# One-hot slot tables of a mixture-of-experts stage: two-byte operands, batches innermost, slot numbers laid out once

## The reference, cut to what matters

```python
capacity = max(1, int(CF * N / E))              # 560 slots of each expert
probs = jax.nn.softmax(xf @ router_w.T, axis=-1)
topw, topi = jax.lax.top_k(probs, K)            # K = 2 experts for each of 3584 tokens
order = jnp.lexsort((-fw, fe))                  # by expert, then by weight
rank = jnp.arange(N * K) - starts[se]
keep = rank < capacity
disp = zeros.at[se, pos].set(xf[st])[:, :capacity]     # the rows of x that each expert gets
g, u = einsum(disp, wg), einsum(disp, wu)
eo = einsum(silu(g) * u, wd)
out = zeros.at[st].add(eo[...] * weight)
```

## Time and profile before

| | us |
|---|---|
| median of 3 runs | 3769.72 |
| lowest, highest | 3767.74, 3772.16 |
| the profiled execution, its own time | 3775.88 |
| its span | 3774.1 |

### The profile page before, as it was taken

How to read it: one execution, slowest core, us unless ns; L and a number is a source line. 1 busy time by engine, 2 the same in 40 slices (tenths; PEclk the granted TensorE clock), 3 DMA queues, 4 the chain that set the end, 5 groups by cost and what they waited for, 6 DMA issues and landing times. The chain is left out here.

```text
span 3774.1 us, 84215 instructions
## 1 busy us (share of the span) xinstructions
PE 3639.7 (96%) x28244; PEld 3139.7 (83%) x28244; DVE 2361.0 (63%) x5543; ACT 1731.9 (46%) x4278; POOL 1305.9 (35%) x1388
## 2 busy tenths in 40 slices
PE   8999999999979999999999999849999999999999
PEld 7888888888868888888888888638998899989998
DVE  6888888888846666666666666576433434434343
ACT  4555555555435555555555555413333333333332
POOL 2333333333325656666556566510101101011010
PEclk9999999999989999999999999869999999999999
DMA  4222222222243434444434343223324334234232
GB/s 127 60 54 63 54 63 53 64 53 64 72 122 94 112 106 104 108 116 107 121 96 113 104 108 97 71 68 94 121 82 122 107 98 123 82 118 123 85 108 69
DMA packets 315057, 349.72 MB, mean 93 GB/s; under 512 B 45308, under 2 KB 232036, under 8 KB 314884
## 3 DMA queue, kind: packets, MB, share of 16 engines
q1 hardware_dynamic: 305796, 318.26, 30.7%
q0 software_dynamic: 9088, 29.17, 2.4%
HBM read 183.23 MB, written 38.91 MB: 59 GB/s over the span
## 5 line engine op out<-in xcount | busy, mean ns | idle before, releaser
L1627 DVE TENSOR_REDUCE x_mx<-x_psS 112x1 f32<-112x752 f32 x512 | 479.7, 937 | 382.2 <-PE x_psS L1180 378.6
L2423 DVE TENSOR_TENSOR hid<-e_psU,act_g 128x280 f32<-128x280 f32 x256 | 115.1, 450 | 622.6 <-PE e_psU L34 585.8
L1462 ACT ACTIVATE x_pt<-x_psE 125x448 f32<-125x448 f32 x768 | 389.6, 542 | 227.6 <-PE x_psE L1192 217.7
L1051 POOL TENSOR_TENSOR part<-x_pt 125x448 f32<-125x448 f32 x255 | 292.4, 1147 | 506.0 <-ACT x_pt L1462 497.1
L2049 POOL DMA_INDIRECT out<-ex_y,sidx x40 | 39.8, 995 | 1020.4 <-DVE ex_y L2457 1010.2
L635 POOL TENSOR_TENSOR qks<-qks,cos 128x448 f32<-128x448 f32 x128 | 148.1, 1157 | 657.0 <-DMA qks<-qk 657.0
L1180 PE MATMUL x_psS<-k_st,q_st 97*112 97x376 f32 x1024 | 287.9, 362 | 24.1 <-DMA k_st<-mk 16.3
L32 PE MATMUL e_psG<-ex_hi,g_hi 128*128 128x280 f32 x1024 | 304.2, 297 | 6.7 <-ACT act_g L2208 4.5
L32 PE MATMUL pj<-xT_hi,win_hi 128*128 128x224 f32 x1024 | 302.2, 295 | 4.0 <-PEq L185 3.9
L2208 ACT ACTIVATE act_g<-e_psG 128x280 f32<-128x280 f32 x256 | 103.7, 405 | 426.4 <-PE e_psG L34 412.1
L1053 POOL TENSOR_TENSOR part<-part,x_pt 125x448 f32<-125x448 f32 x255 | 292.3, 1146 | 20.0
(11 more groups left out here) (305 smaller groups left out, 10890.3 us busy)
## 6 DMA issues: line engine op xcount, KB each, us to landing
k_st<-kT SPq DMA_DIRECT2D x768, 93.8 KB, 2.2
raw_g<-in_L_ffn_wg SPq DMA_DIRECT2D x128, 256.0 KB
raw_u<-in_L_ffn_wu SPq DMA_DIRECT2D x128, 256.0 KB
raw_d<-in_L_ffn_wd SPq DMA_DIRECT2D x128, 256.0 KB
qks<-qk SPq DMA_DIRECT2D x512, 56.0 KB, 2.0
q_st<-qT SPq DMA_DIRECT2D x384, 56.0 KB, 2.0
ctxt<-in_ctx SPq DMA_DIRECT2D x16, 1125.0 KB
xt<-in_x SPq DMA_DIRECT2D x16, 448.0 KB, 3.7
```

Source lines behind the costliest of these rows:

```text
L1051: pool.tensor_tensor(part[:], pt[j][:, 0, :], pt[j][:, 1, :], ALU.add).then_inc(parted, 1)
L1462: act.activation(pt[j][:, i, :], psE[(j + i) % 2][0:KR, 0:2 * T], ACT.Exp, scale=XD ** -0.5).then_inc(exp_done, 1)
L1627: dve.tensor_reduce(mx[:, j, h:h + 1], psS[0:HT, :, 0:376], AX.XY, ALU.max).then_inc(s_taken, 1)
L2423: dve.tensor_tensor(h[ring][:, halves[s]], psU[:, 0:CH], act_g[i][:, halves[s]], ALU.mult).then_inc(S["mul"], 1)
```

## The change

`lo` becomes a two-byte tile (its values, 1 to 128, are exact in bfloat16). A new tile `slot_no` of 128 x 16 two-byte elements on each partition holds the slot numbers, each 16 times in a row; ScalarE writes it once, behind `same`. `onelo` is laid out with the batches innermost, so `one_low` compares two two-byte operands whose innermost step is one element, where before it compared two four-byte operands that were both spread out. In exchange the stationary operand of a table's matmul, 128 adjacent elements before, is now 128 elements that lie 16 elements (32 bytes) apart. VectorE gets one more wait, for ScalarE's copy, ahead of `places`.

```diff
-        hi, lo = (sb("g_" + n, [HT, 2, P]) for n in ("hi", "lo"))
+        hi, lo = sb("g_hi", [HT, 2, P]), sb("g_lo", [HT, 2, P], BF16)
+        slot_no = sb("slot_no", [HT, P, B], BF16)
...
-        onelo = [sb(f"onelo{i}", [HT, B, P], BF16) for i in range(2)]
+        onelo = [sb(f"onelo{i}", [HT, P, B], BF16) for i in range(2)]
...
                     pe.wait_ge(one_ready, 2 * e + i + 1)
                     for b in range(B):
-                        m = pe.matmul(table_place(e), onelo[i][:, b, :], value[:, i, e * B + b, :, :].rearrange("p v t -> p (v t)"),
+                        m = pe.matmul(table_place(e), onelo[i][:, :, b], value[:, i, e * B + b, :, :].rearrange("p v t -> p (v t)"),
...
                 act.activation(same[:], const(C_SAME, P), ACT.Copy).then_inc(same_ready, 1)
+                act.activation(slot_no[:], const(C_IOTA, P)[0:HT].unsqueeze(2).to_broadcast((HT, P, B)), ACT.Copy).then_inc(same_ready, 1)
                 act.activation(act_g[0][:, 0:1], ident[:, 0:1], ACT.Silu)
...
                     if 2 * e + i >= 2:
                         dve.wait_ge(one_used, 2 * e + i - 1)
-                    shape = (HT, B, P)
-                    dve.tensor_tensor(onelo[i][:], lo[:, i, e * B:(e + 1) * B].unsqueeze(2).to_broadcast(shape),
-                                      const(C_IOTA, P)[0:HT].unsqueeze(1).to_broadcast(shape), ALU.is_equal).then_inc(one_ready, 1)
+                    dve.tensor_tensor(onelo[i][:], slot_no[:], lo[:, i, e * B:(e + 1) * B].unsqueeze(1).to_broadcast((HT, P, B)),
+                                      ALU.is_equal).then_inc(one_ready, 1)
...
                 near, far = slice(0, B), slice(B, P)
+                dve.wait_ge(same_ready, 2)
                 places(near)
```

## The result

| | before | after |
|---|---|---|
| median, us | 3770.23 (8 runs) | 3783.61 (8 runs) |
| lowest to highest, us | 3767.74 to 3777.17 | 3778.29 to 3796.47 |
| ratio, 95% interval | | 1.0035 (1.0023 to 1.0047) |
| profiled execution, own time and span | 3775.88, 3774.1 | 3783.97, 3782.2 |

The changed kernel is slower by 0.35%, 13 us, between 9 and 18 by the interval. I had forecast 3768.5 us, in a range of 3764 to 3780. One slow execution is left out of the ratios, 13657 us at a granted clock of 0.48 in the kernel with `lo` doubled; it shifts that kernel's median by less than 0.1 us.

The account below looks back on a forecast made before the run. PE, busy 96% of the span, was taken as the bound. Comparisons -2.1, loads +0.3 and clock +0.6 gave -1.2 us, from a median of 3769.7 to 3768.5 us; range 3764 to 3780 for 8 in 10.

Parts of the forecast that it names:

- VectorE's part: 16 slot-table comparisons of 2048 elements: each falls from 2288 to 1226 ns with two-byte inputs.
- The opening: Start of the experts: two faster comparisons let the second half table and the gathers start 2.1 us earlier.
- ScalarE's part: One copy of 112 x 2048 behind `same`, about 1904 ns, covered by ScalarE's 56.55 us idle time: cost 0.
- the new wait: VectorE's wait at `places` for ScalarE's copy, which ended some 42 us before: cost 0.
- TensorE's part: 256 strided weight loads in the tables: a pair of load and matmul stays at 26 to 28 ns, +0.3 us.
- rival 1: Table loads: each strided column reads its own line, a pair takes 26 ns more; +4.4 us, 3774 us; chance 0.27.
- rival 2: Table loads lose their fast form and go column by column, 77 ns more a pair; 3787 us; chance 0.13.
- "slower": Whole kernel slower by over 0.2%, 7.5 us: rival 2 and the far tail of rival 1; chance 0.15.
- The clock: TensorE's clock may fall before expert 0's first 24 matmuls, costing 0 to 3.2 us; taken as +0.6 us.

Follow-up runs that it names:

- `lo` doubled: Against the changed kernel, `lo` kept twice in a row, slot numbers once, stationary operand contiguous again, comparison still two-byte; 3772.64 us, ratio 0.9996 to before.
- strided load alone: Against the kernel before, only the stationary operand's columns put 32 bytes apart, VectorE still comparing four-byte operands; 3786.58 us, ratio 1.0030.
- groups of two: Against the changed kernel, batches laid out in eight groups of two, stationary columns 4 bytes apart; 3768.95 us, ratio 0.9995 to before.
- the probe: Kernel before with load-and-matmul pairs at column steps 1 to 16 and VectorE comparisons added behind its last work; ran once, 3843.36 us with the probe in it.

## Why the prediction was wrong

- *VectorE's part* was right: 1223 ns for 1226. It had no share in the slowdown: the kernel with the strided load alone is as slow.
- *The opening* was half right. I had 2.1 us for the earlier gather; the traces have 1.6 (11.86 to 10.27). The slower half tables take the rest: with fast loads (groups of two) it is 2.2.
- *ScalarE's part and the new wait* cost nothing, as forecast: the copy ended 42 us ahead of the first reader.
- *TensorE's part* was the step that failed, "I take the value nearest to the instruction's own row, 26 to 28 ns, so +0.3 us". It is 64 ns: 14 half tables, each 0.61 us longer, make 8.5 us, and expert 0 at full clock grew by 8.25 us (157.91 to 166.16). I had argued that the load's 11 ns could double and still hide below 26. But I had it double; a step of 32 bytes touches eight times the lines of a contiguous load, 128 for 16, and the probe shows the load going by lines. My rival 1 had the cause, a line for each column, and too small a price for it (26 ns more a pair, where 36 to 38 came); my rival 2 had the side, with another cause and twice the size; that its limit for "slower", about 64 ns a pair, is what was measured is chance. Its 103 ns was itself read too high: 1.65 us runs to the last result, the 0.41 us beside it to the next start. By the tables' own 0.56 us to the last result it is 68 ns more a pair and 15 us, not 77 and 17.
- *The clock* was known as a term and too small: 0.6 us. In both traces of the changed kernel it fell ahead of expert 0, worth 2.2 us there (168.34 against 166.16 at 1.00). It also fell over the transposes, which I had left out: another 1.0 us (20.49 against 19.49). But the kernel before does it too: its probe version started expert 0 at 0.51 and took 1.6 us longer than the first trace. So it is no property of the change, only perhaps likelier with it; of how many executions fall I have no count, and why it falls where it does stays open.
- *The sum by the traces*, from `g_pos` to expert 0's first addition. With the clock at 1.00 over the first matmuls on both sides: opening -1.9 us (21.37 to 19.49), loads +8.3, together +6.4. With the fall in the changed kernel, as in both its traces, 188.8 us against 179.3 in the first trace of before, +9.6, or against 181.1 in its probe version, +7.8. The three timed comparisons give 13 (9 to 18), 10 (6 to 14) and, for the load alone, 11 us (7 to 15), for which the traces have 8.5 to 10.3. The +9.6 lies in the intervals of both comparisons of the changed kernel, at the low end of the first; the +7.8 lies below the first. Whether something of a few us more is there that no trace showed stays open; the distances in experts 1 to 7 show none.
- Slower by 0.35% had a chance of 0.15 as "slower"; the range ended at 3780.

## What to carry to other kernels

A layout that makes one engine's access adjacent spreads out another's: ask first which engine is the bound. For a two-byte tensor_tensor a run of two adjacent elements was enough for the fast rate, and a column step of two elements cost the weight load nothing, so a layout between the two (groups of two) gave both. In its time that kernel is not to be told from before; in its distances it is 1.8 us shorter (177.5 against 179.3 us to expert 0's first addition). The width of the group should be the smallest that the faster side needs. And a gain of 2 us on the critical path, in a kernel where the start of the stage wanders by 13 us, can be seen in distances between marks of a trace, hardly in its time.

## What the runs showed of the hardware that I had not expected

- The time of a load of 128 two-byte columns goes with the 16-byte lines it touches, 0.45 to 0.52 ns a line, once that is above the 25 ns of a pair; at 0.50 of the granted clock it isn't longer (58 to 62 ns a pair) than at 1.00 (64).
- The granted clock fell while TensorE ran small matmuls without a pause (10 moving columns in the probe): 1.00 from 3771 to 3773 us, 0.80 to 3776, 0.50 from there. It was back at 0.98 from 3785 on, 3.3 us into the pairs with 128 moving columns. One trace shows it.
- A step of 32 bytes on all three operands of a two-byte tensor_tensor took 8928 ns for 2048 elements, 3.9 times the 2292 ns of the slow form with unit steps on the output.
